# Two buffers for the moved sine products and norm parts made on the turned columns, in a sandwich of two attention stacks and a scan

## The reference

```python
for i in range(DEPTH):                                  # DEPTH = 6
    x = attn_layer(shift_tokens(x), Wqkv[i], q_scale[i], k_scale[i], Wo[i]) + x
    x = ffn_layer(shift_tokens(x), ln_g[i], ln_b[i], W1[i], b1[i], W2[i], b2[i]) + x
...
def attn_layer(x, Wqkv, qs, ksc, Wo):                   # 16 heads of 64
    q, k, v = split(x @ Wqkv)
    q = l2norm(q) * qs
    k = l2norm(k) * ksc
    q = q * cos * scale + rotate_half(q) * sin * scale
    k = k * cos * inv + rotate_half(k) * sin * inv
    out = local_attention(q, k, v)                      # windows of 32, each sees itself and the one before
    return out @ Wo
...
x = x + 0.5 * ffn_stack(layernorm(x)); x = x + scan_block(layernorm(x)); x = x + 0.5 * ffn_stack(layernorm(x))
```

## Time and profile before

| | |
|---|---|
| runs, median of 3 | 3472.9 us (3462.06 to 3480.17) |
| the profiled execution, own time | 3464.47 us |
| its span | 3462.7 us |
| granted TensorE clock, mean | 0.951 |
| TensorE busy over the span | 87% |
| VectorE busy | 87% |
| GpSimd busy | 70% |
| ScalarE busy | 54% |
| TensorE / VectorE / GpSimd busy in 300 to 1400 us | 1022 / 1009 / 844 us of 1100 us |

### The profile page before, as it was taken

How to read it: one execution, slowest core, us unless ns; L and a number is a source line. 1 busy time by engine, 2 the same in 40 slices (tenths; PEclk the granted TensorE clock), 3 DMA queues, 4 the chain that set the end, 5 groups by cost and what they waited for, 6 DMA issues and landing times. The chain is left out here.

```text
span 3462.7 us, 132411 instructions
## 1 busy us (share of the span) xinstructions
PE 3018.9 (87%) x58280; PEld 1846.3 (53%) x58280; DVE 3005.4 (87%) x4152; ACT 1870.6 (54%) x3502; POOL 2437.8 (70%) x1679
## 2 busy tenths in 40 slices
PE   5789998999999999987666689998999999999997
PEld 3455555555555555553323455555555655555553
DVE  5689999889999999987897789989999999899984
ACT  2355555556556565556663355655555555565553
POOL 2568777777787787775463568778777787787773
PEclk7889999999999999998898899999999999999998
DMA  4223333333332333320002223333333333333320
GB/s 126 68 67 80 75 88 77 75 90 74 80 93 68 87 89 70 83 68 28 10 7 52 66 69 80 78 88 76 76 92 70 80 95 70 80 88 74 82 69 14
DMA packets 114726, 251.06 MB, mean 73 GB/s; under 512 B 27244, under 2 KB 60648, under 8 KB 114152
## 3 DMA queue, kind: packets, MB, share of 16 engines
q1 hardware_dynamic: 114152, 242.60, 29.6%
HBM read 38.02 MB, written 3.15 MB: 12 GB/s over the span
## 5 line engine op out<-in xcount | busy, mean ns | idle before, releaser
L1241 POOL TENSOR_TENSOR k_ring<-k_ring,partner 128x512 f32<-128x512 f32 x384 | 492.1, 1281 | 619.6 <-DMA partner<-sines 603.4
L1077 ACT ACTIVATE squares<-general 128x512 f32<-128x512 f32 x768 | 447.5, 605 | 783.4 <-PE general L650 781.6
L856 DVE SCALAR_TENSOR_TENSOR sines<-general,vec,consts 128x512 f32<-128x512 f32 x768 | 558.6, 727 | 133.8 <-ACT squares L1077 119.9
L1261 POOL TENSOR_TENSOR probs<-probs,row_sum 128x1024 f32<-128x1024 f32 x192 | 365.7, 1904 | 190.9 <-DVE row_sum L947 189.7
L1241 POOL TENSOR_TENSOR q_ring<-q_ring,partner 128x512 f32<-128x512 f32 x384 | 494.6, 1288 | 0.0
L684 PE MATMUL general<-probs_t,v_buf 32*64 32x64 f32 x24576 | 366.6, 234 | 143.8 <-DVE probs L930 55.1
L684 PEld LDWEIGHTS general<-probs_t,v_buf 32*64 32x64 f32 x24576 | 314.8, 134 | 305.3 <-issue 282.3
L648 PE MATMUL general<-xs_hi,wqkv_lo 128*128 128x512 f32 x768 | 394.4, 514 | 24.6 <-DVE k_ring L862 11.5
L1255 POOL TENSOR_TENSOR probs<-probs,q_scale 128x1024 f32<-128x1024 f32 x192 | 371.1, 1933 | 11.9
L1247 POOL TENSOR_TENSOR probs<-probs,row_max 128x1024 f32<-128x1024 f32 x192 | 379.0, 1974 | 0.0
L1139 ACT ACTIVATE att<-general 128x256 f32<-128x256 f32 x768 | 232.3, 389 | 260.6 <-PE general L684 260.1
(11 more groups left out here) (231 smaller groups left out, 6203.3 us busy)
## 6 DMA issues: line engine op xcount, KB each, us to landing
partner<-sines SPq DMA_DIRECT2D x1536, 128.0 KB
wqkv_raw<-in_wqkv SPq DMA_DIRECT2D x80, 208.0 KB, 2.8
wo<-in_wo SPq DMA_DIRECT2D x12, 512.0 KB, 5.6
w<-in_w SPq DMA_DIRECT2D x12, 341.0 KB, 3.2
base_dram<-x SPq DMA_DIRECT2D x8, 256.0 KB, 2.4
att<-in_wqkv SPq DMA_DIRECT2D x2, 1024.0 KB, 6.5
sines<-base_dram SPq DMA_DIRECT2D x8, 256.0 KB, 3.8
w<-in_w SPq DMA_DIRECT2D x12, 128.0 KB
```

What stands on the lines that cost most here:

```text
L856: e.scalar_tensor_tensor(out=by_seq(sines[:, i % 2, which, :]), in0=g, scalar=scale, in1=both(tables[:, 2 * which + 1, :]), op0=ALU.mult, ...
L1077: e.activation(squares[:, (2 * p + which) % 4, :], general_of(("proj", k, n, p, which))[:, :], ACT.Square).then_inc(S[f"squared_{side}"], 1)
L1241: e.tensor_tensor(y, y, partner[:, which, :], ALU.add).then_inc(S[f"rotated_{side}"], 1)
L1261: e.tensor_tensor(y, y, spread_keys(row_sum[:, i % 2, :]), ALU.mult).then_inc(S["probs_done"], 1)
```

## The change

Two parts, with the order of the pieces on every engine as it was.

First, `partner` gets two slots, by `i % 2`, and the semaphore `moved` becomes `moved0` and `moved1`. The DMAs of pair i now wait until GpSimd has rotated pair i - 2, not pair i - 1, and still until both sine products of pair i are written.

Second, the high and low parts of one over the norm are made on the columns before they are turned back (128x128, not 128x512). VectorE copies the root to fp32r (high) and subtracts (low), each waiting for the one before; ScalarE's second root of 128x128 and VectorE's L917 are gone, and ScalarE's copy after the turn writes `inv_parts` itself. The selectors of the spreading matmul share columns (640 where there were 1024); the matmuls and their shapes stay.

```diff
-        partner = sb("partner", [P, 2, COLS])
+        partner = sb("partner", [P, 2, 2, COLS])
...
         def move_partners(e, w, k, n, p):
             w.wait_ge(S["sin_q"], i + 1)
             w.wait_ge(S["sin_k"], i + 1)
-            w.wait_ge(S["rotated_q"], i)
-            w.wait_ge(S["rotated_k"], i)
+            w.wait_ge(S["rotated_q"], i - 1)
+            w.wait_ge(S["rotated_k"], i - 1)
             for r in range(0, P, WIN):
                 to = r + WIN if r % DH == 0 else r - WIN
-                e.dma_start(partner[to:to + WIN, :, :], sines[r:r + WIN, i % 2, :, :]).then_inc(S["moved"], 16)
+                e.dma_start(partner[to:to + WIN, i % 2, :, :], sines[r:r + WIN, i % 2, :, :]).then_inc(S[f"moved{i % 2}"], 16)
...
         def dve_norms_back(e, w, k, n):
             m = k * ITEMS + n
             w.wait_ge(S["k_root"], m + 1)
+            root, low, high = (norm_t[:, :, i * NORM_ROWS:(i + 1) * NORM_ROWS] for i in range(3))
+            e.tensor_copy(high.bitcast(F32R), root).then_inc(S["norms_high"], 1)
+            w.wait_ge(S["norms_high"], m + 1)
+            e.tensor_tensor(low, root, high, ALU.subtract).then_inc(S["norms_low"], 1)
+            w.wait_ge(S["norms_low"], m + 1)
             w.wait_ge(S["inv_parts"], m)
             e.transpose(inv_norm[:, :], norm_t.rearrange("p w h -> p (w h)")).then_inc(S["k_norms_turned"], 1)
-        def dve_norms_low(e, w, k, n):
-            w.wait_ge(S["inv_hi"], m + 1)
-            w.wait_ge(S["norm_spread"], m * GROUPS)
-            e.scalar_tensor_tensor(out=inv_parts[:, :], in0=inv_hi[:, :].bitcast(F32), scalar=low_rows, in1=inv_norm[:, :],
-                                   op0=ALU.mult, op1=ALU.add).then_inc(S["inv_parts"], 1)
...
-            e.activation(norm_t[:, :, NORM_ROWS:2 * NORM_ROWS], norm_t[:, :, 0:NORM_ROWS], ACT.Sqrt).then_inc(S["q_scaled"], 1)
-            w.wait_ge(S["q_scaled"], (m + 1) * 9)
+            w.wait_ge(S["q_scaled"], (m + 1) * 8)
             e.activation(norm_t[:, :, 0:NORM_ROWS], norm_t[:, :, 0:NORM_ROWS], ACT.Sqrt).then_inc(S["k_root"], 1)
...
         def act_norms_high(e, w, k, n):
             w.wait_ge(S["k_norms_turned"], m + 1)
-            w.wait_ge(S["inv_parts"], m)
-            e.activation(inv_hi[:, :], inv_norm[:, :], ACT.Copy).then_inc(S["inv_hi"], 1)
+            w.wait_ge(S["norm_spread"], m * GROUPS)
+            e.activation(inv_parts[:, :], inv_norm[:, :], ACT.Copy).then_inc(S["inv_parts"], 1)
...
         def pool_rotate(e, w, k, n, p, which):
-            w.wait_ge(S["moved"], 64 * (i + 1))
+            w.wait_ge(S[f"moved{i % 2}"], (i // 2 + 1) * 64)
             w.wait_ge(S[f"cos_{side}"], i + 1)
-            e.tensor_tensor(y, y, partner[:, which, :], ALU.add).then_inc(S[f"rotated_{side}"], 1)
+            e.tensor_tensor(y, y, partner[:, i % 2, which, :], ALU.add).then_inc(S[f"rotated_{side}"], 1)
```

More of the change, by code:

```diff
@@ L57 @@
 C_IDENT, C_CENTER, C_MEAN, C_SUMSEL = 0, P, 2 * P, 2 * P + 1
-C_LOW = C_SUMSEL + 64
-C_TABLES = C_LOW + 1
+C_TABLES = C_SUMSEL + 64
 C_STAY = C_TABLES + 4 * SEQ
@@ L62 @@
 C_SPREAD = C_MASK + NWIN * 2 * WIN
-C_END = C_SPREAD + 2 * GROUPS * P
+C_END = C_SPREAD + GROUPS * (P + WIN)
 V_QS, V_KS, V_G, V_B, V_B2, V_BA, V_BG, V_END = 0, 1, 2, 3, 4, 5, 8, 11
@@ L357 @@
 shifted raw0_loaded raw1_loaded raw2_loaded first_loaded wqkv_hi wqkv_lo wo_loaded w1_loaded w2_loaded
-xs_hi xs_lo proj_q proj_k squared_q squared_k cos_q cos_k sin_q sin_k moved rotated_q rotated_k
-squares_summed sums_kept sums_turned sums_inverted q_scaled k_root k_norms_turned inv_hi inv_parts
+xs_hi xs_lo proj_q proj_k squared_q squared_k cos_q cos_k sin_q sin_k moved0 moved1 rotated_q rotated_k
+squares_summed sums_kept sums_turned sums_inverted q_scaled k_root norms_high norms_low k_norms_turned inv_parts
 v_projected v_kept norm_spread k_inv_kept scored k_norms_off row_max max_off q_norms_off exponent row_sum row_inv
@@ L399, in macaron_kernel @@
         xs_lo = sb("xs_lo", [P, 2, COLS], F32R)
-        spread_sel = sb("spread_sel", [P, 2, GROUPS * P], F32R)
+        spread_sel = sb("spread_sel", [P, GROUPS, P + WIN], F32R)
         wo = sb("wo", [P, PAIRS, P])
@@ L412, in macaron_kernel @@
         k_inv = sb("k_inv", [P, WIN + COLS])
-        inv_hi, inv_parts = sb("inv_hi", [P, COLS], F32R), sb("inv_parts", [P, COLS], F32R)
+        inv_parts = sb("inv_parts", [P, COLS], F32R)
         att = sb("att", [P, PAIRS, COLS])
@@ L558, in sync_stack @@
                 w.wait_ge(S[f"base{c}_stored"], 16 * (k + 1))
-                w.wait_ge(S["moved"], 64 * (k + 1) * ITEMS * PAIRS)
+                for i in range(2):
+                    w.wait_ge(S[f"moved{i}"], 32 * (k + 1) * ITEMS * PAIRS)
                 e.dma_start(base[c], base_dram[:, c * COLS:(c + 1) * COLS]).then_inc(S[f"base{c}_loaded"], 16)
@@ L724, in pe_spread @@
             for seq in range(CHUNK_SEQS):
-                sel, cut = spread_sel[:, seq, group * P:(group + 1) * P], slice(seq * SEQ, (seq + 1) * SEQ)
+                sel, cut = spread_sel[:, group, seq * WIN:seq * WIN + P], slice(seq * SEQ, (seq + 1) * SEQ)
                 done = e.matmul(g[:, cut], sel, inv_parts[:, cut], start=True, stop=True)
@@ L813, in vector_program @@
             e.tensor_copy(mask_bf[:, :], recast[:, 0:C_SPREAD - C_MASK])
-            e.tensor_copy(spread_sel[:, :, :], recast[:, C_SPREAD - C_MASK:C_END - C_STAY].rearrange("p (s c) -> p s c", s=2))
+            e.tensor_copy(spread_sel[:, :, :], recast[:, C_SPREAD - C_MASK:C_END - C_STAY].rearrange("p (g c) -> p g c", g=GROUPS))
             w.wait_ge(S["consts_loaded"], 16)
@@ L853, in dve_rotate @@
             w.wait_ge(S[f"squared_{side}"], i + 1)
-            w.wait_ge(S["moved"], 64 * (i - 1))
+            w.wait_ge(S[f"moved{i % 2}"], i // 2 * 64)
             e.scalar_tensor_tensor(out=by_seq(sines[:, i % 2, which, :]), in0=g, scalar=scale, in1=both(tables[:, 2 * which + 1, :]),
@@ L1001, in vector_stack @@
                     dve_root(e, w, ("ffn", k, st.root))
-                if st.norms_back is not None:
-                    dve_norms_low(e, w, k, st.norms_back)
                 if st.scale:
@@ L1646, in constants @@
     c[np.arange(P), C_SUMSEL + 30 + np.arange(P) // DH] = 1
-    c[np.arange(P) % WIN // NORM_ROWS == 1, C_LOW] = -1
     half = np.arange(0, DH, 2, dtype=f)
@@ L1667, in constants @@
     c[:, C_MASK:C_SPREAD] = np.where(seen, f(0), f(-1e30)).reshape(P, -1)
-    for head in range(HEADS):
-        for seq in range(CHUNK_SEQS):
-            at = C_SPREAD + seq * GROUPS * P + (head // 4 * 4 + (head - seq) % 4) * WIN
+    for group in range(GROUPS):
+        for q in range(5):
+            head, at = 4 * group + q % 4, C_SPREAD + group * (P + WIN) + q * WIN
             row = norm_row(head // 2, 1) + head % 2
-            c[row, at:at + WIN] = c[row + NORM_ROWS, at:at + WIN] = 1
+            c[row + NORM_ROWS, at:at + WIN] = c[row + 2 * NORM_ROWS, at:at + WIN] = 1
     return c
```

4 lines of the change are left out of this document (1 added, 3 removed).

## The result

The changed kernel takes 3378.2 us (median of 4 runs, 3374.9 to 3384.0), beside 3467.5 us for the kernel before in the same comparison (3455.9 to 3480.2): a ratio of 0.974 [0.970, 0.978], 89 us less. The profiled execution has 3381.3 us and a span of 3379.5, 83.2 us under the span of before.

The account below looks back on a forecast made before the run. No engine was full; TensorE's three stalls per item, behind a VectorE chain from p = 6 to p = 1, were taken as the bound. Terms of -24 and +2.5 gave -21 us: 3443 profiled, 3452 median, range 3388 to 3500.

Parts of the forecast that it names:

- Four items fill and drain the stacks; I give them nothing.: At the ends of the stacks: four of the 48 items were counted with no gain.
- 34 items by -0.7: Items without weight splits, fill or drain: each gains 0.7 us, between 0.5 and 1.0, for -24 us.
- the pair at 2.3 us: VectorE's new copy and subtraction at p = 1, both blocked by GpSimd, make the turn 2.3 us later.
- TensorE's three named stalls: Per item, at p = 6 for L930, p = 0 for L862, p = 2 for squares of k: together 159 us.
- The ten items with weight splits: Items beside loads of a new layer, where GpSimd also splits weights: +0.25 us each, +2.5 us.
- I am wrong if ScalarE's copy waits long for the turn: Sign against the forecast: ScalarE's copy at the norms waiting long for VectorE's turn; no size given.
- About half of the 603 us to stay: GpSimd's wait for the moved sine products, 603.4 us before: about half was expected to remain.
- The count against the rule: Norms' part: least durations give VectorE 1.1 us an item; the shared-port rule trades one blocked operation for two.
- Larger gain: Rival, chance 0.20: with GpSimd ahead, TensorE's three stalls (159 us) halve, -80 us, 3393.
- Given back: Rival, chance 0.27: the turn's delay eats L885's lead, the square of k comes when it came, 3465 to 3480.
- Slower: Rival, chance 0.17: the turn about 1.0 us late and L885 still blocked, 44 items by +0.9, +40 us, 3513.

Follow-up runs that it names:

- norms alone: The changed kernel with the old order of moves, each waiting again for the rotation of the pair just before: 3421.6 us, 0.990 of the kernel before.
- split behind the scores: The kernel before, with VectorE's L885 put behind the score multiplications of p = 6 instead of ahead of them: 3452.0 us, 0.999.
- filler: The kernel before with 228 matmuls repeated that change nothing (centrings, and the first product of k at p = 0): 3455.8 us, 1.001.
- moves alone: The kernel before with the two slots and semaphores for the moves, and the norms made as before: 3369.1 us, 0.976.

## Why the prediction was wrong

My sum had -21 us for the profiled execution; -83.2 were measured. Of the 62 us between, about 25 came at the ends of the stacks, 27 with the clock, and 10 in the 38 items (-31 at full clock, where I had -24 and +2.5).

**The step that failed: "Four items fill and drain the stacks; I give them nothing."** They gave about 25 of 83 us. In the first item the projections come with little other work, and the loop of rotation, move and rotation sets the pace. GpSimd's k rotations there, before:

```profile
71.53 1.28 POOL L1241 TENSOR_TENSOR k_ring<-k_ring,partner 128x512 f32<-128x512 f32 x1 [5.10 <-DMA partner<-sines]
...
78.41 1.27 POOL L1241 TENSOR_TENSOR k_ring<-k_ring,partner 128x512 f32<-128x512 f32 x1 [4.35 <-DMA partner<-sines]
...
85.22 1.27 POOL L1241 TENSOR_TENSOR k_ring<-k_ring,partner 128x512 f32<-128x512 f32 x1 [4.32 <-DMA partner<-sines]
```

and after:

```profile
71.00 1.29 POOL L1236 TENSOR_TENSOR k_ring<-k_ring,partner 128x512 f32<-128x512 f32 x1 [2.79 <-DMA partner<-sines]
...
73.97 1.28 POOL L1236 TENSOR_TENSOR k_ring<-k_ring,partner 128x512 f32<-128x512 f32 x1 [0.46 <-DMA partner<-sines]
...
77.83 1.26 POOL L1236 TENSOR_TENSOR k_ring<-k_ring,partner 128x512 f32<-128x512 f32 x1 [1.36 <-DMA partner<-sines]
```

Before, 6.8 us a pair: 2.5 us for two rotations and 4.3 us for the move behind them. I had the 4.7 us of a move in the earlier trace rows and read it only where GpSimd has slack. The kernel with early moves in the first items alone shows it by itself: 29 us less.

**The term that was missing: the clock.** I had read 0.951 and 0.98 and left them out of the sum. About 27 us of the 83 are items that no longer fall to half clock. Here is one of before, TensorE's timeline and then windows of it (length, busy times by engine, then the granted clock):

```profile
604.93 5.49 PE L747 MATMUL general<-centered,w 128*128 128x512 f32 x6 [2.35 <-POOL centered L1227]
```

```profile
600.00:604.00 4.00, 2.58 (x73) 1.93 (x73) 3.88 (x7) 1.19 (x2) 3.92 (x3) 1.00 0.59 134
604.00:606.00 2.00, 1.07 (x2) 0.55 (x3) 2.00 (x4) 1.98 (x6) 1.73 (x3) 0.52 0.01 2
606.00:610.00 4.00, 4.00 (x6) 1.49 (x5) 2.85 (x4) 3.79 (x12) 3.39 (x3) 0.50 0.29 66
610.00:614.00 4.00, 4.00 (x10) 1.67 (x9) 2.17 (x3) 3.03 (x5) 1.50 (x2) 0.89 0.29 68
```

TensorE stands still for 2.35 us, and the gates behind it run at 1.2 GHz, not 2.4. In those 38 items the clock falls 17 times before, each within 1.3 us of the end of a stop of 1.14 to 2.35 us; after, once. The stops themselves changed:

| stops of TensorE in the 38 items | 1.1 to 1.3 us | 1.3 to 1.7 | 1.7 and more | falls of the clock |
|---|---|---|---|---|
| before | 39 | 17 | 15 | 17 |
| norms alone | 35 | 19 | 11 | 7 |
| split behind the scores | 40 | 3 | 10 | 11 |
| filler | 12 | 7 | 4 | 3 |
| moves alone | 47 | 8 | 1 | 4 |
| changed | 70 | 7 | 0 | 1 |

The table counts one profiled execution of each kernel; the repeat of the changed kernel has 3 falls, not 1. A stop of 1.1 to 1.3 us was beside a fall 7 times of 39 before, but once of 70 in the changed kernel, and one of 1.7 or more 7 times of 15. So a stop's own length does not decide it. What the falls cost is mostly the slower matmuls: in the 19 items with time at half clock TensorE is busy 58.53 us each and idle 4.64, in the 19 others busy 57.29 and idle 4.40, so 1.24 of the 1.5 us are the clock and 0.24 are longer waits. The runs of the kernel before agree, of which there are 17, 17 and 11 on the three chips: on each chip a line laid through their times and clocks has 22 to 27 us less for 0.01 more of granted clock (correlation -0.67 to -0.82), and 0.951 to 0.961 is that step.

So the early moves paid twice: for the stops, and for the clock that fell beside them. That the clock can be had back by TensorE's own work and stops, without any of the change, is shown by the filler, which leaves the orders and semaphores of before. It both shortens the stops and adds work; which of the two keeps the clock was not separated. The Trainium skill, "TensorE: Matmul & The Clock Gate", section "HAM oscillation — how this bites in real kernels", describes the clock falling back in the waits between bursts of matmuls. Its case is a kernel whose wait for a DMA after each burst is longer than the burst. The trace agrees in kind only: here the stops beside the falls are 1.14 to 2.35 us, in a stream that is over 90% busy.

**"34 items by -0.7"** was right in size: -0.81 us measured at full clock, over 38 items. So were the durations that it was built from: L885 at 0.68 us, L901's median from 1.22 to 0.43, the pair at 2.3 us. But the size is in part luck. The term was meant to come out of TensorE's three named stalls, and in an item at full clock these gave 0.2 us only: 1.23 + 1.04 + 0.38 = 2.65 before, 0.39 + 1.06 + 1.01 = 2.46 after. The stall for the scores (at the values of p = 6) fell as forecast, and that for the squares took nearly all of it back. The other 0.6 us are waits that I had put into no term (0.5; L707's and L648's above all) and busy time (0.1). So "TensorE's stalls per item are three" was short of some: the scores (L707) and the projection's first product (L648) waited too, 14.9 and 11.5 us. A smaller slip: by its row L909 ended at 2551.10, not 2551.0, so its lead on L1114 was 0.9 us. The ten items with weight splits, which I had put at a loss of 0.25 us, gained at least like the rest: of the 38 items the 16 with such splits on GpSimd went from 62.90 to 61.05 us, the 22 others from 62.09 to 60.80.

**"I am wrong if ScalarE's copy waits long for the turn"** was itself wrong. It waits 42.0 us in 47 waits, and the squares cost 33.7 us more than before. But TensorE comes earlier by more than that.

**"About half of the 603 us to stay"**: 464 us stayed. GpSimd comes earlier and waits for sines that are not yet written.

**The count against the rule.** I had written that by least durations alone VectorE would gain 1.1 us from the norms' part, and by the rule of the Trainium skill on the shared ports ("SBUF — State Buffer", "Who interferes with whom") trade one blocked operation for two. Both are right, each in its kernel: the new pair takes 0.22 and 0.29 us where GpSimd waits (norms alone), 0.99 and 1.27 where it runs, as the rule has it. At full clock the norms' part gains 0.65 us an item by itself and costs 0.15 on top of the moves (60.88 against 60.73), beside the 14 us in the first items. In the whole kernel this doesn't show: the ratios are 0.974 (0.975 in the repeat) and 0.976, each with an interval of 0.002 or more to either side.

**The rivals.** "Larger gain" came nearest in time (3393), and for another reason than its own: the three stalls did not halve. "Given back" was at the right place: the stall for the squares grew by 33.7 us, but that took back only what the stall for the scores had lost (38.2 us), and not the rest. "Slower" did not come near.

**Left open.** What makes the clock fall at one stop and not at the next was not tried. The falls differ from one execution to the next of the same kernel (its mean clock is 0.947 to 0.958 in the 45 runs of before on the three chips), so the 27 us belong to the two profiled executions. Why the stalls of L707 and L648 went with the change, and why the first items lose with the norms' part, was not tried either.

## What to carry to other kernels

Ask of a loop that hides in the steady state (here rotation, move, rotation: 6.8 us) where the work that hides it is missing: at the ends of a stack it is the pace. Look at the granted clock beside TensorE's idle time: here its falls cost a third of what the change gained, and 10 of 17 lay beside stops of 1.3 us and more. And two dependent VectorE operations within SBUF, at a place where GpSimd has work, can wait for a GpSimd instruction each: here 0.22 and 0.29 us of work took 0.99 and 1.27. Moving the first to ScalarE gave 20 us.

## What the runs showed of the hardware that I had not expected

- The granted clock falls to half beside single stops of 1.14 to 2.35 us, in stretches where TensorE is busy 93% of the time (1022 of 1100 us), and an item with such a fall takes 1.5 us longer (63.17 against 61.69), 1.24 of it in TensorE's busy time.
- 228 more matmuls, 77 us of them, left the time of the kernel within 0.3%: the clock stayed up (0.962 against 0.951 in the profiled executions), and TensorE's busy time rose by only 34.7 us.
- ScalarE writes the fp32r high part of a 128x128 tile as a root in about 0.31 us (0.308 to 0.312 in all 48) and is never hindered there; the same rounding as a copy on VectorE takes 0.22 us alone and 0.99 beside GpSimd.
